# A Perceiver layer on one core: the score tiles of head 0 in runs of four inside the projection, and products of the identity where TensorE stands still

## The reference

```python
x = x + cross_attention(layernorm(x), ctx_768)      # 512 queries, 8192 keys, 16 heads of 32, then an MLP
x = x + local_attention(layernorm(x))               # 512 tokens, causal window of 256
x = x + fp4_ffn(layernorm(x))                       # weights and activations rounded to FP4 in blocks of 16
...
q = x @ Wq + bq;  k = y @ Wk + bk;  v = y @ Wv + bv # y = ctx_768, 8192 x 384; q, k, v 512 wide
attn = softmax(q k^T / sqrt(32));  out = attn v     # per head
```

## Time and profile before

| | us |
|---|---|
| median of 3 runs | 1532.03 |
| the runs | 1530.37 to 1534.92 |
| the profiled execution, its own time | 1528.88 |
| its span, first to last instruction | 1526.9 |

### The profile page before, as it was taken

One profiled execution on the slowest core, in us unless ns is written; L12 is line 12 of the kernel. 1 busy time (PEld: TensorE's weight loads), 2 busy tenths in 40 slices (PEclk: granted clock), 3 DMA queues, 4 the chain that ended last, 5 costly groups with the idle time before them and its releaser, 6 DMA issues. The chain is left out here.

```text
span 1526.9 us, 38954 instructions
## 1 busy us (share of the span) xinstructions
PE 1350.8 (88%) x16544; PEld 705.2 (46%) x16544; DVE 1158.4 (76%) x1834; ACT 815.0 (53%) x1530; POOL 792.0 (52%) x307
## 2 busy tenths in 40 slices
PE   6966878797759999999999999999999997885798
PEld 3422434343325555655555555555555443363354
DVE  7654766676658888888888888888888745676797
ACT  3422333333327777777776777767776841475211
POOL 3211111111128999999999999999999201100111
PEclk8988899899979999999999999999999998999899
DMA  6554465655652512122212212122211030590000
GB/s 225 164 140 113 130 183 166 184 137 170 168 144 62 173 61 63 35 62 61 64 45 63 62 61 63 35 63 64 70 39 52 4 132 0 110 202 1 0 8 21
DMA packets 127645, 137.41 MB, mean 90 GB/s; under 512 B 44977, under 2 KB 108849, under 8 KB 125425
## 3 DMA queue, kind: packets, MB, share of 16 engines
q1 hardware_dynamic: 127472, 134.93, 31.3%
HBM read 75.66 MB, written 44.17 MB: 78 GB/s over the span
## 5 line engine op out<-in xcount | busy, mean ns | idle before, releaser
L1235 DVE TENSOR_REDUCE early<-attend_banks 128x1 f32<-128x512 f32 x960 | 617.3, 685 | 89.1 <-PE attend_banks L976 83.9
L1196 ACT ACTIVATE attend_prob<-attend_banks 128x512 f32<-128x512 f32 x1024 | 535.9, 599 | 201.1 <-PE attend_banks L1020 198.7
L1384 POOL TENSOR_TENSOR early<-early,attend_prob 128x1024 f32<-128x1024 f32 x210 | 619.8, 2951 | 36.3 <-ACT attend_prob L1196 8.3
L1031 PE MATMUL attend_banks<-attend_prob,attend_vh 128*32 128x512 f32 x2048 | 269.1, 593 | 0.0
L1020 PE MATMUL attend_banks<-early,k_first 97*32 97x512 f16 x2560 | 261.9, 384 | 3.4 <-ACT attend_prob L1196 3.4
L976 PE MATMUL attend_banks<-k_first,early 96*32 96x512 f16 x2304 | 241.8, 387 | 6.8 <-DMA attend_fold<-in_c_fold_dram 6.8
L1020 PE MATMUL attend_banks<-early,attend_k_rest 97*32 97x512 f16 x1536 | 155.5, 381 | 2.8 <-ACT attend_prob L1196 2.8
L976 PE MATMUL attend_banks<-attend_k_rest,early 96*32 96x512 f16 x1536 | 157.9, 380 | 0.0
L465 POOL TENSOR_TENSOR project_w_whole<-project_grid,project_qscale 128x704 f32<-128x704 f32 x24 | 33.2, 1385 | 236.3 <-DVE project_grid L588 236.3
L1042 PE MATMUL attend_banks<-attend_prob,ones 128*32 128x128 f32 x3048 | 135.4, 272 | 3.7 <-DVE attend_recip L1247 3.7
L1042 PEld LDWEIGHTS attend_banks<-attend_prob,ones 128*32 128x32 f32 x3048 | 97.7, 110 | 52.6 <-DVE attend_recip L1247 11.2
(11 more groups left out here) (176 smaller groups left out, 1830.6 us busy)
## 6 DMA issues: line engine op xcount, KB each, us to landing
v_scratch<-project_v SPq DMA_DIRECT2D x16, 1024.0 KB, 5.3
attend_vh<-v_scratch SPq DMA_DIRECT2D x16, 1024.0 KB, 4.9
early<-in_ctx_dram SPq DMA_DIRECT2D x16, 768.0 KB, 7.2
k_first<-k_scratch SPq DMA_DIRECT2D x36, 256.0 KB, 3.4
k_scratch<-project_k_hi SPq DMA_DIRECT2D x64, 128.0 KB, 2.8
k_scratch<-project_k_lo SPq DMA_DIRECT2D x64, 128.0 KB, 3.0
attend_k_rest<-k_scratch SPq DMA_DIRECT2D x24, 256.0 KB, 3.5
k_first<-k_scratch SPq DMA_DIRECT2D x36, 128.0 KB, 3.6
```

Source lines behind the costliest of these rows:

```text
L1031: last = nc.tensor.matmul(pv_ps[t * HD:(t + 1) * HD, :], vh[:, s, BT * q + t, :], prob[:, q % PSLOTS, t, :], start=q == 0, stop=q == QUADS ...
L1196: nc.scalar.activation(prob[:, q % PSLOTS, t, :], s_ps[:, s_bank[BT * q + t]], ACT.Exp, scale=SCALE).then_inc(p_ready, 1)
L1235: nc.vector.tensor_reduce(part_max[:, s, j, part:part + 1], pre_ps[:, bank], AX.X, ALU.max).then_inc(pre_read, 1)
L1384: nc.gpsimd.tensor_tensor(sums, sums, prob[:, q % PSLOTS, 0:n], ALU.add).then_inc(pool_summed, 1)
```

## The change

1. **Runs of four.** `part_at` gives each block at most two places for a whole part: `VALUES_1` (after the second value group) in blocks 2 to 14, `KEYS_0` (after the first key group) in blocks 3, 8 and 10, `KEYS_2` and `VALUES_2` in the last block. A run is four tiles into four banks, three of `yT_ps` and `pre_ps`, with no wait between them. Before a run TensorE waits for the last block's transposes to be read by VectorE (`ylo_ready`) and for the tiles before (`pre_read`); `next_y` waits for the three `yT_ps` tiles of the run before it.
2. **Head 1's first eight tiles** move from the head of the attend stage into blocks 8 and 10 (`KEYS_0`, their keys loaded after pair 2). `first_pre` is gone, and TensorE's steps of attend begin with head 0.
3. **VectorE's order**: `maxima` of a run stand together, and the weight steps are split 3, 2 and 2 (or 3) around them.
4. **The last pair**: block 15's keys go between the second and third value groups of block 14.
5. **Loads and stores**: the copies into `k_first` come before the stores to `k_scratch`; `fold` is loaded at the start; most of head 0's values (56 of 64 tiles) are loaded before the stage ends; the waits for all stores at the start of attend are moved to where they are needed.
6. **`keep_busy`**: 123 products of the f32 128x128 identity with itself, in seven places: 6 before and 9 after the first transposes, 10 at the end of project, 10 at the end of attend, 16 at the start of local, 16 before its scores, 56 at the start of ffn. Nobody reads them.
7. ScalarE loads the table of the exponential at the end of project (`warm`).

```diff
@@ both sides: score tiles
-            PLACES = 2 * G
-            tiles_at = {(b, at): [] for b in range(NB) for at in range(PLACES)}
...
-            def pre_bank(n):
-                turn = n - (len(tile_order) - LAST_BLOCK_TILES)
-                return pre_ps[:] if turn < 0 or turn % 4 == 0 else yT_ps[:, turn % 4 - 1]
...
+            KEYS_0, KEYS_2, VALUES_1, VALUES_2 = range(4)
+            part_at = {(2, VALUES_1): (0, 0), (3, KEYS_0): (0, 1), (3, VALUES_1): (0, 2), (8, KEYS_0): (1, 0), (10, KEYS_0): (1, 1)}
+            for b in range(4, NB - 1):
+                part_at[b, VALUES_1] = (0, b - 1)
+            part_at[NB - 1, KEYS_2] = (0, NB - 2)
+            part_at[NB - 1, VALUES_2] = (0, NB - 1)
+            done_before = {at: TT * n for n, at in enumerate(sorted(part_at))}
+            def pre_bank(j):
+                return yT_ps[:, j] if j < TT - 1 else pre_ps[:]
+            def tiles_before(b):
+                return sum(TT for at in part_at if at < (b, VALUES_1))
@@ TensorE, project
+        def keep_busy(bank, times):
+            for _ in range(times):
+                nc.tensor.matmul(bank[:, 0:P], ident[:], ident[:], start=True, stop=True)
...
+                keep_busy(pre_ps, 6)
                 turn_y(16, 0)
+                keep_busy(pre_ps, 9)
...
+                        if h == 0:
+                            pe.wait_ge(k_out[part % 2], 16 * K_OUTS * (part // 2 + 1))
+                        elif part == 0:
+                            pe.wait_ge(k_in[1][0], 32)
+                        pe.wait_ge(ylo_ready, min(b + (2 if place == VALUES_1 else 1), NB))
+                        wait(pe, pre_read, done_before[b, place])
+                        for j in range(TT):
+                            nc.tensor.matmul(pre_bank(j), q_stack[0:KROWS, h, j * P:(j + 1) * P],
...
                 def next_y(i, u):
                     wait(pe, ylo_ready, 2 * i + u + 1)
+                    wait(pe, pre_read, tiles_before(2 * i + u) - 1)
...
-                values(i, 0)
+                values(i, 0, range(2))
                 keys(i, 1)
+                values(i, 0, range(2, BT))
                 values(i, 1)
+                pe.wait_ge(khi_ready, NB * G)
+                keep_busy(k_ps[:, 0], 10)
@@ VectorE, project
+                    def keys(u):
+                        b = 2 * i + u
                         for g in range(G):
                             key_low(i, u, g)
...
+                            if g < 3:
+                                quantize(1)
+                            if g >= 1:
+                                maxima(b, KEYS_0, range(2 * g - 2, min(2 * g, TT)))
+                        maxima(b, KEYS_2)
...
                             y_low(i, u)
+                            quantize(2)
+                            maxima(2 * i + u, VALUES_1)
+                            if last:
+                                keys(1)
+                            quantize(2 + u)
+                            if last:
+                                quantize(5)
+                                maxima(2 * i + 1, VALUES_2)
@@ attend, local, ffn
-                for k in range(FIRST_TILES):
-                    first_pre(k)
...
+                pe.wait_ge(h_low, FM)
+                keep_busy(banks[:, h_bank[TT]], 10)
...
+                keep_busy(t_ps[:, 0], 16)
                 pe.wait_ge(xn_ready, 2 * TT)
...
+                keep_busy(o_ps[:, 0], 16)
                 pe.wait_ge(v_read, TT)
...
+                keep_busy(y_ps[:, 1], 56)
                 turn("x", 0)
```

More of the change, by code:

```diff
@@ L227, in perceiver @@
         ones_row = sem("ones_row")
+        fold_in = sem("fold_in")
+        v_in = [sem(f"v_in{s}") for s in range(2)]
         K_OUTS = 2 * HG + 3
@@ L509, in y_high, with values_out @@
                     nc.scalar.activation(yT_hi[:, 1 - u], yT_ps[:], ACT.Copy).then_inc(yhi_ready, 1)
-                def values_out(i, u):
-                    for t in range(BT):
+                def values_out(i, u, tiles=range(BT)):
+                    for t in tiles:
                         wait(act, v_ready, (2 * i + u) * BT + t + 1)
@@ L596, in halves, with maxima @@
                                                    op0=ALU.mult, op1=ALU.subtract).then_inc(halved, 1)
[L598 to L603 removed]
+                def maxima(b, place, tiles=range(TT)):
+                    if (b, place) in part_at:
+                        h, part = part_at[b, place]
+                        for j in tiles:
+                            dve.wait_ge(pre_ready, done_before[b, place] + j + 1)
+                            nc.vector.tensor_reduce(part_max[:, h, j, part:part + 1], pre_bank(j), AX.X,
+                                                    ALU.max).then_inc(pre_read, 1)
                 STEPS = []
@@ L691, in keys, with values @@
                         last.then_inc(k_ready, 1)
-                        maxima(2 * i + u, g)
-                def values(i, u):
-                    if isinstance(i, int) and i == 0 and u == 0:
+                        if g in (0, 2):
+                            maxima(2 * i + u, (KEYS_0, None, KEYS_2)[g])
+                def values(i, u, tiles=range(BT)):
+                    if i == 0 and u == 0:
                         pe.wait_ge(wsplit_hi, 2)
                         pe.wait_ge(wsplit_lo, 2)
-                    for t in range(BT):
+                    for t in tiles:
                         n = (2 * i + u) * BT + t
@@ L803, in perceiver @@
             den_ps = banks[:, DEN_BANK]
-            fold_in = sem("fold_in")
             rest_ones = sem("rest_ones")
-            v_in = [sem(f"v_in{s}") for s in range(2)]
             pre_ready = sem("pre_ready")
@@ L1193, in head @@
                             act.wait_ge(dve_summed, min(q + 1 - PSLOTS, LAST_SUMMED))
+                        if first and q == 2:
+                            for u in range(2):
+                                act.wait_ge(k_out[u], 16 * K_OUTS * NB // 2)
                         for t in range(BT):
```

180 lines of the change are left out of this document (81 added, 99 removed).

## The result

The changed kernel takes 1457.05 us (median of 4 runs, 1455.47 to 1458.94) against 1532.3 us for the kernel before on the same chip (4 runs, 1530.37 to 1534.92). The ratio is 0.9508, with a 95% interval of 0.9489 to 0.9528. The gain is 75.2 us; 80.8 were predicted, and 1452 as the time. The profiled span is 1453.5 us, 73.4 less than before, at a mean clock of 0.973 against 0.949.

What follows compares the result with a forecast made beforehand. Waits between TensorE and VectorE, for score-tile reductions and the weight unit's load, bound the projection. Savings 22.8 + 4.8 + 27 + 21.7 + 1.5 + 1 + 2 = 80.8 us give 1452; 8-in-10 range 1432 to 1482.

Steps and rivals of the forecast that it cites:

- usual pairs: Projection pairs 2, 3 and 6: TensorE's run waits for `y_low`; each falls from 49.1 to 41.5 us, saving 22.8 together.
- pairs 4 and 5: Projection pairs also holding head 1's runs: transposes wait for the third tile's reduction; 46.7 us each, 4.8 us saved together.
- L: The moment a pair's gate weights land in the projection, from which the prediction counts; next one expected 41.5 us later.
- the walk: Step-by-step timing of a usual pair from L: `y_low` ends at L + 8.7, last value group out at L + 33.5.
- Pair 1: Projection's pair 1: no stall for the stacked queries, fewer waits on one bank in block 3; 27 us saved of 67.6.
- Seam: Last pair to attend's first exponential: stores by readiness, `fold` there, eight tiles gone; exponential at L + 41.2, 21.7 us saved.
- Identity products: Filler products keeping the clock up: 0.25 us each; 1.5 us saved at the start, 2 later, between -6 and +9.
- a warmer start: Head 0 at attend's beginning: begins at a warmer clock, 1 us saved.
- that rival: VectorE late in every second block too, perhaps through its port lock with GpSimd: 30 us kept, 1481; chance 0.17.
- the first rival: The gate load's wait doesn't bind: usual pairs about 36 us, pairs 4 and 5 40, time 1421; chance 0.07.
- the rival: Identity products overrun their waits at 0.38 us each, in ffn and elsewhere: +13 us, 1464; chance 0.13.
- the slower way: Transposes wait for maxima in both blocks of each projection pair: 56 us a pair, 1559; chance 0.03.

Runs made afterwards that it cites:

- the last experiment: Changed kernel with early unit loads, head 1's first eight tiles back in attend, identity products only at the start and 44 instead of 56 in ffn: 1410.65 us, ratio 0.9204.

## Why the prediction was right, and where its sizes were off

**Direction and mechanism.** The time lay in the range and 5 us above the forecast. Its main step held: the single bank was what TensorE waited for. One bank takes all of the gain away (1538). That four banks need the placement, since the transposes and `y_low` use the same ones, is argued from the program. What was to be late next was late next: `y_low` behind the gate load in usual pairs, and the third reduction of head 1's run in pairs 4 and 5. Early loads took the first away and the return of the eight tiles the second.

**Usual pairs: predicted 41.5, measured 42.7, 41.5 and 42.5** from one L to the next (124.95, 167.65, 209.16; 302.46, 344.97). Two sizes were low. From the start of the run to the value store are 25.7 us in pairs 2 and 6 and 24.9 in pair 3; the walk had 23.1 and 1.7 for the clock, 24.8. So the clock costs 1.8 to 2.6 after the stall, by difference; I had taken 1.7 of a bound of 2.4, and 2.6 is above the bound. And the gate weights landed 9.2 us after the store in pair 2, in the other five pairs 7.8 to 8.2 (8.0 predicted).

**Pairs 4 and 5: predicted 46.7.** Measured 46.6 and 46.7 (209.16, 255.75, 302.46). The stall was 8.2 and 8.5 us.

**Pair 1: 27 predicted, 25.1 measured.** The run after the query stands behind other work, as said. What was mis-sized is block 3: the wait for the third tile of `KEYS_0` is 3.45 us (3.0 predicted), and I had put the clock behind it at nothing: the transposes take 1.71 us instead of 1.47, and the seven products behind them start 0.43 us apart instead of 0.216, 1.5 us more.

**Seam: 21.7 predicted, 21.3 measured.** `y_low` ends at L + 8.7 and the exponential starts at L + 41.3, against L + 41.2. The account of the saving was less exact than its sum. The 6.81 us for `fold` were 2.5 of `fold` and the rest, by the trace, the barrier that SP's stores held up. The table load of ScalarE for the exponential, 1.28 us, which stands ahead of the first one before and now runs at 380.53 in ScalarE's idle time, I had not counted by name. One sign that I had named was missed: the first exponential was to be near 380 us and is at 386.24. Its way there was to save 77.8 us and saves 71.5; 3.2 of the difference are pairs 2 to 6, 1.9 pair 1, 0.8 the start and 0.4 the seam.

**Identity products.** Their price was bounded rightly: 0.225 us, at the lower bound of 0.22 from the f32 pace (what the prediction calls 30 products are instructions, two to a product). I took 0.25. The Trainium skill, "TensorE: Matmul & The Clock Gate", section "Back-to-back issue gap", would make a product of 128 columns dearer by its weight load, an estimate of 0.31 us by its ratio. By that estimate 56 products would take 17.4 us; the trace has 12.7, so it doesn't hold for these f32 products. Their worth was set too high. By the medians it can't be told from nothing. At the start the whole stretch to pair 1 gained 0.7 us. In local the transposes take 1.09 us instead of 1.97, but they start 7.1 us after attend's last product (1200.8) where they started 5.8 after it before, since the ten delay the barrier; from that product to local's last one it is 130.15 us after and 129.96 before. The 1.2 us of the table for local and ffn are luck: what I had counted on came to nothing, and 1.7 us came from the group near the end of ffn, which I had not named. Nor is it shown that head 0 gained by a warmer start: from the first exponential to local's last product are 944.7 us with the identity products, 944.4 without them, and 945.1 before.

**The rivals.** VectorE isn't late in any second block of pairs 2 to 6, neither in the changed kernel nor, at 36.5 us a pair, in the faster ones. What that rival named as its mechanism, VectorE and GpSimd shutting each other out, no run tests. The load binds. The price that the first rival gave for pairs without the load's wait was right for the usual ones (36 us); pairs 4 and 5 take 44, not 40. The products overrun in ffn by 2.8 us, which the last experiment took back; at 13 us the rival was far too dear. The sign for it, transposes later than 15 us after local's last product, wasn't reached: they start 13.8 us after its end. Nothing went the slower way, but its mechanism is there in small: the transposes wait for the maxima in pairs 4 and 5.

## What to carry to other kernels

When one engine's work is moved off a wait, walk every queue again from the event that is late (here the landing of a load) and ask what is late next: that gave 46.7 us for a pair to within 0.1, closer than the 1.2 us by which the usual pairs differ among themselves, so part of it is luck. Then ask whether the event itself can be moved: the change left an issue order in place that was worth 30 us more with no other work touched. Filler products for the clock gave back in ffn 2.9 us right behind them and took 2.8 by overrunning, and over the whole kernel nothing that can be measured; count them to the wait and no further, and try the kernel without them.

## What was not expected of the hardware

An f32 product of the identity with 128 columns is two instructions that start 0.112 us apart, though each has a weight load of 0.192 us on record:

```profile
L273 PEld LDWEIGHTS ffn_yf_ps<-ident 128*128 128x128 f32 x112 | 12.6, 192 | 1.7 <-issue 1.7
```

192 ns x 112 would be 21.5 us, and 12.6 are busy: on record the loads overlap each other as well as the products. The clock behind a stall of TensorE, in the changed kernel but for the first: after 3.19 us the transposes ran at the upper level, after 3.45 they took 1.71 us instead of 1.47, after 4.66 the run took 1.44 instead of 0.81, after 8.19 the transposes 2.79. But the length of the stall alone doesn't set the loss: in the kernel with early loads the same transposes of pair 1 took 2.46 us after 3.46. What else does, no run shows.
